# Maxima of the first unit sent through DRAM in two halves, and all steps of a planned kernel put in a new order

## The chip, the cores and the metric

The kernel runs on one core of one Trainium2 chip, as one program. The metric is the device time of one execution in microseconds (us). A core has five engines that run side by side, each its own instructions in a fixed order: TensorE (PE, matmuls), VectorE (DVE), ScalarE (ACT), GpSimd (POOL) and SyncE (SP, which here only issues DMAs). They wait for each other through semaphores.

## The reference

Four sequences (batches) of 1024 tokens by 128 features pass through eight blocks with residual adds; the last kind comes twice:

```python
x = x + _L0_attn_a_ref(_layernorm(x, axis=-1), ...)   # full attention, 16 heads of 8
x = x + _L0_ffn_ref(_layernorm(x, axis=-1), ...)
x = x + _L0_attn_b_ref(_layernorm(x, axis=-1), ...)   # causal, then local attention
x = x + _L0_ffn_ref(_layernorm(x, axis=-1), ...)
x = x + _L1_attn_a_ref(_layernorm(x, axis=-1), ...)   # window of 32, padded
x = x + _L1_ffn_ref(_layernorm(x, axis=-1), ...)      # 8 experts, 2 for each token
x = x + _L1_attn_b_ref(_layernorm(x, axis=-1), ...)   # window of 128 and 4 sinks
x = x + _L1_ffn_ref(_layernorm(x, axis=-1), ...)
```

Every attention ends in a softmax over the keys and a product with the values. The part that the change edits is in the full one:

```python
x_h = x.reshape(b, t, h, d).transpose(0, 2, 1, 3)
xw = jnp.einsum('bhtd,hde->bhte', x_h, w_att_val)
att = jnp.einsum('bhte,bhse->bhts', xw, x_h) / jnp.sqrt(jnp.asarray(d, x.dtype))
att = jax.nn.softmax(att, axis=-1)
...
o = jnp.einsum('bhts,bhsd->bhtd', att, vx)
```

## The kernel before

**Stages.** Batches are b0 to b3. Each goes through nine stages: full attention, ffn1, causal, local, ffn2, padded, moe1, sink, moe2. The stages of different batches overlap; the full attention of b0 and then that of b2 run in the first 500 us. In a moe stage the chosen tokens are gathered into 23 tiles of 128 slots (in DRAM, `scr_y`), and three matrices of an expert (`WB`, 384 KB a load) are loaded for each tile.

**One attention.** Full attention has four units of four heads, u0 to u3. For a unit the planner adds these steps:

- `load` (SP, L1819 and L1821): queries and keys from DRAM into one buffer each of the rings `QO` and `KO`, of four buffers each; 792 KB in four DMAs. It waits until the buffers' last readers are done.
- `maxima`: 32 steps "top", each four score matmuls (PE, L1102) and one maximum over them (DVE, L1532). 16 of them are for the unit's first two heads (hp 0), 16 for its last two (hp 1). Then `tops` (DVE, L1538, into `MTa`), `tops_turn` (a transpose on PE, L1109, and four operations on DVE that end in L1551, into `MTd`), `tops_out` (SP, L1839, `MTd` to DRAM, 24 KB) and `tops_in` (SP, L1848, two DMAs from DRAM into three more rows of `QO`). So the scores come out with their maximum taken off.
- `attend`: two halves (of the queries), each 16 steps "scores" (four matmuls on PE, L1122, and one exponential on ACT, L1295) and eight products with the values (PE, L1139). Each half ends with an ACT copy into `OB` (L1301) and a `divide` (PE L1149, DVE).

Tops and scores share a ring of three pairs of PSUM banks (`RB`). So maxima of the next unit run between scores of this one, one top taken with every score or two; a "pure stretch" of tops is one in which PE has no scores of the unit before left.

**What sets the order.** A planner (`Plan`, `streams`) takes the steps one by one with costs written into the code, and writes a fixed list for each engine. The tables `LEADS` (by stage) and `URGENT` (by kind of step) shift how early a step wants to be taken; `SHORT` and `WORTH` weigh which engine's steps go first and a step's use of a ring. On the chip each engine runs its list in order, and a waiting instruction holds up all behind it. That holds for the queue of SP too, which issues the loads, `tops_out`, `tops_in`, the loads of `WB`, and `zero` (L1855), one DMA of 1518 KB for each batch that clears `scr_y`. The sink attention of a batch (in the last quarter of the program) has units of the same steps on other shapes; its first top of a unit comes with mask matmuls (L1082).

## Time and profile before

| | |
|---|---|
| median of three runs | 2473.16 us (2466.74 to 2474.1) |
| profiled execution | 2472.5 us, span 2470.7 us |
| mean granted TensorE clock | 0.947 of full |
| PE busy | 2166.9 us, 88% of the span |
| DVE busy | 1653.9 us, 67% |
| ACT busy | 1440.0 us, 58% |
| POOL busy | 661.4 us, 27% |

The span runs from the first to the last instruction; the device time of the same execution is 1.8 us longer. A busy share is an average over stages: in the first 340 us DVE (maxima) and ACT (exponentials) work beside PE, and in the last 600 us PE waits for weights and for other engines at times.

### The profile page before, as it was taken

What the parts mean: (1) busy time and instruction counts of PE and PEld (TensorE: products, weight loads), DVE (VectorE), ACT (ScalarE), POOL (GpSimd) and SP (SyncE); (2) the same over time, 40 slices, a digit from 0 to 9 for tenths busy, and PEclk for the clock granted to TensorE, in tenths of its full rate; (3) what the DMA queues carried; (4) which work ended last, traced back from release to release, by engine and by line L of the source; (5) the groups of instructions that cost most, each with busy time, mean ns of one, the idle gap of its engine ahead of it and who ended that gap; (6) DMA issues with size and microseconds to landing.
All of it is one profiled execution on the core that took longest, in us unless ns stands there. A gap on an engine that the chain in (4) does not pass through costs nothing.

```text
span 2470.7 us, 61917 instructions
## 1 busy us (share of the span) xinstructions
PE 2166.9 (88%) x25853; PEld 1229.8 (50%) x25874; DVE 1653.9 (67%) x3651; ACT 1440.0 (58%) x2121; POOL 661.4 (27%) x597
## 2 busy tenths in 40 slices
PE   5588898789988999999898998899989889989987
PEld 2111231133322433423565446767857788766886
DVE  7888788776688777413745357675667576676545
ACT  1177657667887578799665774455344334344432
POOL 2400010020010202011233333433435364233563
PEclk8599999899999999999999999999999899989999
DMA  5600100111011111111222135535334666324576
GB/s 163 232 15 29 40 13 17 40 47 31 25 51 50 52 32 54 31 50 31 66 74 72 22 103 153 153 88 156 117 84 122 208 208 194 95 85 125 175 231 208
DMA packets 156238, 231.06 MB, mean 94 GB/s; under 512 B 19504, under 2 KB 79408, under 8 KB 155704
## 3 DMA queue, kind: packets, MB, share of 16 engines
q1 hardware_dynamic: 140952, 202.69, 28.1%
...
## 4 chain that ended last, share of the span: by engine, by line
PE 50%; DVE 19%; DMA 11%; ACT 7%; issue 6%; POOL 4%; SPq 3%; ACTq 0%; DVEq 0%; POOLq 0%
PE PS L1139 11%; DVE MS L1532 11%; PE PS L1188 6%; PE PS L1122 6%; ACT PT L1295 6%; PE PS L1102 5%; DMA scr_y<-XN,SL 3%; PE PS L1205 3%; PE PS L1089 3%; PE PS L1001 2%; PE PS L1011 2%; PE PS L972 2%; DMA WB<-in_mW 2%; PE PS L1082 2%; POOL scr_y L1756 2%
## 5 line engine op out<-in xcount | busy, mean ns | idle before, releaser
L1295 ACT ACTIVATE PT<-PS 128x1024 f32<-128x1024 f32 (+3 forms) x1216 | 1026.8, 908 | 399.5 <-PE PS L1122 392.0
L1532 DVE TENSOR_REDUCE MS<-PS 128x2 f32<-128x1024 f32 (+4 forms) x736 | 787.8, 1099 | 236.1 <-PE PS L1102 232.7
L1139 PE MATMUL PS<-PT,VA 128*9 128x512 f32 (+9 forms) x6720 | 571.3, 438 | 8.0 <-ACT PT L1295 6.2
L1122 PE MATMUL PS<-QO,KO 51*64 51x512 bf16 (+11 forms) x6304 | 444.4, 311 | 44.9 <-ACT PT L1295 16.1
L1102 PE MATMUL PS<-KO,QO 48*64 48x512 bf16 (+2 forms) x3520 | 302.9, 340 | 84.0 <-DVE MS L1532 70.8
L1122 PEld LDWEIGHTS PS<-QO,KO 51*64 51x64 bf16 (+3 forms) x6304 | 185.8, 107 | 238.7 <-ACT PT L1295 84.8
L1188 PE MATMUL PS<-SG,WB 128*128 128x128 f32 x2208 | 286.7, 283 | 16.8 <-DMA WB<-in_mW 14.4
L1102 PEld LDWEIGHTS PS<-KO,QO 48*64 48x64 bf16 (+1 forms) x3520 | 131.5, 107 | 337.4 <-DVE MS L1532 186.4
L1188 PEld LDWEIGHTS PS<-SG,WB 128*128 128x128 f32 x2208 | 269.1, 197 | 24.9 <-DMA WB<-in_mW 16.5
L1764 POOL DMA_INDIRECT scr_o<-SG,TO x184 | 181.5, 986 | 248.8 <-ACT SG L1337 226.0
L1317 ACT ACTIVATE HM<-PS 128x384 f32<-128x384 f32 x184 | 90.2, 490 | 224.9 <-PE PS L1188 224.9
L1139 PEld LDWEIGHTS PS<-PT,VA 128*9 128x9 f32 (+3 forms) x6720 | 127.0, 90 | 177.0 <-issue 121.8
L1089 PE MATMUL PS<-c_half 64*64 64x128 bf16 (+4 forms) x2560 | 170.3, 286 | 43.9 <-ACT PT L1295 15.3
L1654 DVE SCALAR_TENSOR_TENSOR HM<-HM,PS 128x384 f32<-128x384 f32 x184 | 101.2, 550 | 123.7 <-ACT HM L1317 123.2
L1205 PE MATMUL PS<-W,HM 128*128 x1104 | 160.4, 285 | 19.8 <-DVE HM L1656 9.8
L1756 POOL DMA_INDIRECT scr_y<-XN,SL x128 | 124.6, 974 | 194.1 <-DMA scr_y<-XN,SL 93.1
L1704 POOL MEMSET VA<- 128x32 f32 (+2 forms) x20 | 3.8, 190 | 643.7 <-PE PS L1139 643.7
L1089 PEld LDWEIGHTS PS<-c_half 64*64 64x64 bf16 x2560 | 65.5, 105 | 194.7 <-ACT PT L1295 96.2
L1205 PEld LDWEIGHTS PS<-W,HM 128*128 128x128 f32 x1104 | 139.9, 195 | 30.9 <-issue 29.6
L1301 ACT ACTIVATE OB<-PS 128x512 f32<-128x512 f32 x144 | 84.8, 599 | 92.5 <-PE PS L1139 89.5
L1561 DVE RECIPROCAL RC<-PS 128x16 f32<-128x16 f32 x144 | 36.3, 252 | 148.0 <-PE PS L1149 147.7
L1234 ACT ACTIVATE XT<-PS 128x512 f32<-128x512 f32 (+2 forms) x128 | 71.6, 593 | 90.0 <-PE PS L972 89.7
(166 smaller groups left out, 2377.1 us busy)
## 6 DMA issues: line engine op xcount, KB each, us to landing
...
```

Of the source, the lines that this page charges most:

```text
L1089: mm(pb[64 * c:64 * c + 64, h2, at:at + copies * width], C["identw"][r, :], rows, start=i == 0, stop=False, skip_group_check=True)
L1102: p = mm(pb[c:c + n, h2, at:at + kn], q[:, 128 * tt + c:128 * tt + c + n], k[:, k0:k0 + kn], start=not masked, stop=True, skip_group_check ...
L1122: p = mm(pb[c:c + n, h2, at:at + tn], k[:, k0 + c:k0 + c + n], q[:, t0:t0 + tn], start=not masked, stop=True, skip_group_check=masked)
L1139: p = mm(bank[32 * h:32 * h + D + 1, c0:c0 + tn], va[0:kn, :], pt[0:kn, h % 2, at:at + tn], start=s["first"] and j == 0, stop=s["last"] an ...
L1188: p = mm(pb[:, k, 128 * c:128 * c + 128], wt[:, at:at + 128], y, start=True, stop=True)
L1205: p = mm(RA[s.use["bank"].i][:, 0:128], hm[:, 128 * c:128 * c + 128], W3[:, bass.ds(first + 128 * c, 128)], start=c == 0, stop=c == 2)
L1295: e = activation(pt[0:r, :, a:b], ps[0:r, :, a:b], ACT.Exp, scale=s["A"].scale)
L1317: activation(HM[s.use["hm"].i][:, :], RB[s.use["bank"].i][:, 0, 0:DW], ACT.Tanh, scale=0.5).then_inc(S["up_tanh"], 1)
L1532: v.tensor_reduce(to, got, AX.X, ALU.max).then_inc(S["top"], 1)
L1654: last(v.scalar_tensor_tensor(hm, hm, 1.0, pb[:, 0, 0:DW], ALU.add, ALU.mult))
L1756: p.indirect_dma_start(scr_y[b], bass.IndirectOffsetOnAxis(ap=SL[b][:, c, i:i + 1], axis=0), XN[:, i, 0:ROW], None).then_inc(S[s.signals[" ...
L1764: p.indirect_dma_start(scr_o[b], bass.IndirectOffsetOnAxis(ap=TO[b][:, t:t + 1], axis=0), SG[s["yt"].i][:, at:at + 128], None).then_inc(S[ ...
```

## The change

It has two parts. First, for unit u0 of b0 alone, the maxima are sent in two halves: after the 16 tops of two heads come a `tops`, a `tops_turn`, a `tops_out` and a `tops_in` of their own, on 16 rows instead of 32, and then the same again for the other two heads. Scores of a pair of heads wait only for their own `tops_in`. All other units wait as before. Second, the tables have other numbers, so that the order of steps on all engines is another one.

```diff
--- before.py
+++ after.py
@@ -17,11 +17,11 @@
 RS8 = float(8.0) ** -0.5
 INF = float("inf")
 HOP = 200.0
-LEADS = dict(full=(1132, -776, 406, -1439), ffn1=(-3117, -525, 2830, 2001), causal=(1089, -1943, -1344, -1890), local=(-1543, 777, -158, 647), ffn2=(-197, 3580, -615, -1022), padded=(-948, -510, -413, -182), moe1=(2339, -1699, 271, -906), sink=(556, 567, -1777, 1297), moe2=(2401, -2034, -4275, -134))
...
-SHORT = dict(pe=2339.0, act=1281.0, dve=653.0, pool=2521.0, sp=24300.0)
+LEADS = dict(full=(715, -319, 616, -1226), ffn1=(-3511, -187, 2610, 2331), causal=(1741, -1760, -1442, -1611), local=(-1557, 1080, 559, 503), ffn2=(277, 3502, -765, -1049), padded=(-858, -449, -354, -310), moe1=(2599, -1691, 527, -724), sink=(348, 595, -1796, 1382), moe2=(2448, -2203, -3913, -26))
...
+SHORT = dict(pe=100.0, act=1260.0, dve=653.0, pool=3206.0, sp=24467.0)
 ISSUE = 500.0
-SWITCH, WORTH = 95.0, 285706.0
+SWITCH, WORTH = 95.0, 80724.0
 ENGINES = ("pe", "act", "dve", "pool", "sp")
 SLOT_TILES, GROUP, ROW = 23, 4, 132
 STAGES = ("moe1", "moe2")
@@ -459,16 +459,24 @@
                     s.use["tk"].give(s["top"])
                     top.append(s["top"])
                     U["read"].append(s["top_mm"])
-            s = add("tops", [("dve", 200, "tops")], dict(top=top), dict(mt=MT), A=A, ms=ms)
-            ms.give(s["tops"])
+                if U["halves"]:
+                    U["m"].append(sent_tops(A, U, top, ms, hp, hp == 1))
+                    top = []
+            if not U["halves"]:
+                U["m"] = [sent_tops(A, U, top, ms, None, True)] * 2
+
+        def sent_tops(A, U, top, ms, hp, last):
+            s = add("tops", [("dve", 200, "tops")], dict(top=top), dict(mt=MT), A=A, ms=ms, hp=hp)
+            if last:
+                ms.give(s["tops"])
             mt = s.use["mt"]
-            s = add("tops_turn", [("pe", 200, "tops_mm"), ("dve", 1150, "tops_split")], dict(tops=[s["tops"]]), dict(bank=RA), mt=mt)
+            s = add("tops_turn", [("pe", 200, "tops_mm"), ("dve", 1150, "tops_split")], dict(tops=[s["tops"]]), dict(bank=RA), mt=mt, hp=hp)
             s.use["bank"].give(s["tops_split"])
-            s = add("tops_out", [("sp", ISSUE, "")], dict(tops=[s["tops_split"]], m=state["m"]), b=b, dmas=lambda s: [("m_out%s" % b, 1, 2200, 100)])
+            s = add("tops_out", [("sp", ISSUE, "")], dict(tops=[s["tops_split"]], m=state["m"]), b=b, hp=hp, dmas=lambda s: [("m_out%s" % b, 1, 2200, 100)])
             mt.give(s["dma"])
-            s = add("tops_in", [("sp", 2 * ISSUE, "")], dict(m=[s["dma"]]), A=A, U=U, b=b, dmas=lambda s: [("q_in%s" % U["qo"].i, 2, 2200, 200)])
+            s = add("tops_in", [("sp", 2 * ISSUE, "")], dict(m=[s["dma"]]), A=A, U=U, b=b, hp=hp, dmas=lambda s: [("q_in%s" % U["qo"].i, 2, 2200, 200)])
             state["m"] = [s["dma"]]
-            U["load"] = U["load"] + [s["dma"]]
+            return s["dma"]
 
         def attend(A, U, va, v_ready, o):
             done, read = [], []
@@ -482,7 +490,7 @@
                     for hp in range(2):
                         s = add("scores", [("pe", score_mms([x[3] for x in g["blocks"]], A.tiled, masked), "scores"),
                                            ("act", sum(on_act(2 * (x[2] - x[1])) for x in g["exps"]), "exp")],
-                                dict(load=U["load"]), dict(bank=RB, pt=PT, **chain) if po is None else dict(bank=RB, pt=PT),
+                                dict(load=U["load"] + U["m"][hp:hp + 1]), dict(bank=RB, pt=PT, **chain) if po is None else dict(bank=RB, pt=PT),
                                 leaves=dict(PT=1 - hp), A=A, U=U, g=g, hp=hp, po=po, behind=behind, mode=mode(A.tiled))
                         po, behind, fc = s.use.get("po", po), s.use["pt"], s.use.get("fc", fc)
                         s.use["bank"].give(s["exp"])
@@ -518,7 +526,7 @@
                     takes["o"] = O
                 s = add("load", [("sp", ISSUE * n, "")], dict(q=state["q"][:u + 1], k=state["k"][:u + 1], ones=ones_in if A.tops else []), takes, A=A, b=b, u=u, o=o,
                         dmas=lambda s, n=n: [("q_in%s" % s.use["qo"].i, n, 2000, 1300)])
-                U = dict(u=u, qo=s.use["qo"], qo2=s.use.get("qo2"), ko=s.use["ko"], load=[s["dma"]], read=[])
+                U = dict(u=u, qo=s.use["qo"], qo2=s.use.get("qo2"), ko=s.use["ko"], load=[s["dma"]], read=[], m=[], halves=A.name == "full" and b == 0 and u == 0)
                 if "rest" in state:
                     state.pop("rest")([s["dma"]])
                 if A.name == "full" and u == 2:
@@ -852,6 +860,11 @@
              half=("identb", "identw", "mC", "mL", "mA", "mB", "mBt", "mBt1", "below", "onesb"))
 
 
+def heads_of(s):
+
+    return slice(0, 32) if s["hp"] is None else slice(16 * s["hp"], 16 * s["hp"] + 16)
+
+
 def program(nc, d, places, out, scr, scr_m, scr_y, scr_o):
     ctx = ExitStack()
     with ctx:
@@ -1106,7 +1119,9 @@
             def tops_turn(s):
                 w.wait_all(s.needs["tops"])
                 w.wait_all(s.use["bank"].after)
-                nc.tensor.transpose(RA[s.use["bank"].i][0:32, 0:128], MTa[:, :], ident[:, :]).then_inc(S["tops_mm"], 1)
+                r = heads_of(s)
+                n = r.stop - r.start
+                nc.tensor.transpose(RA[s.use["bank"].i][0:n, 0:128], MTa[:, 0:n], ident[:, :]).then_inc(S["tops_mm"], 1)
 
             def scores(s):
                 w.wait_all(s.needs["load"])
@@ -1534,21 +1549,24 @@
             def tops(s):
                 w.wait_all(s.needs["top"])
                 w.wait_all(s.use["mt"].after)
+                r = heads_of(s)
                 if s["A"].name == "full":
-                    v.tensor_tensor(MTa[:, :], MS[:, :, 0], MS[:, :, 1], ALU.max).then_inc(S["tops"], 1)
+                    v.tensor_tensor(MTa[:, 0:r.stop - r.start], MS[:, r, 0], MS[:, r, 1], ALU.max).then_inc(S["tops"], 1)
                 else:
                     v.tensor_copy(MTa[:, :], MS[:, :, 0]).then_inc(S["tops"], 1)
 
             def tops_turn(s):
                 w.wait_ge("tops_mm", s.signals["tops_mm"].value)
-                top = RA[s.use["bank"].i][0:32, 0:128]
-                last(v.tensor_scalar(MTd[:, 0, :], top, -1.0, None, ALU.mult))
-                settled()
-                last(v.scalar_tensor_tensor(MTc[:, :], top, -1.0, MTd[:, 0, :], ALU.mult, ALU.subtract))
-                settled()
-                last(v.tensor_copy(MTd[:, 1, :], MTc[:, :]))
-                settled()
-                v.tensor_tensor(MTd[:, 2, :], MTc[:, :], MTd[:, 1, :], ALU.subtract).then_inc(S["tops_split"], 1)
+                r = heads_of(s)
+                n = r.stop - r.start
+                top = RA[s.use["bank"].i][0:n, 0:128]
+                last(v.tensor_scalar(MTd[0:n, 0, :], top, -1.0, None, ALU.mult))
+                settled()
+                last(v.scalar_tensor_tensor(MTc[0:n, :], top, -1.0, MTd[0:n, 0, :], ALU.mult, ALU.subtract))
+                settled()
+                last(v.tensor_copy(MTd[0:n, 1, :], MTc[0:n, :]))
+                settled()
+                v.tensor_tensor(MTd[0:n, 2, :], MTc[0:n, :], MTd[0:n, 1, :], ALU.subtract).then_inc(S["tops_split"], 1)
 
             def divide(s):
                 A, u, half = s["A"], s["U"]["u"], s["half"]
@@ -1836,14 +1854,18 @@
             def tops_out(s):
                 w.wait_all(s.needs["tops"])
                 w.wait_all(s.needs["m"])
-                eng.dma_start(scr_m[s["b"]].rearrange("a r t -> r a t"), MTd[:, :, :]).then_inc(S[s.signals["dma"].name], 16)
+                r = heads_of(s)
+                eng.dma_start(scr_m[s["b"]][:, r, :].rearrange("a r t -> r a t"), MTd[0:r.stop - r.start, :, :]).then_inc(S[s.signals["dma"].name], 16)
 
             def tops_in(s):
                 A, U, got = s["A"], s["U"], S[s.signals["dma"].name]
                 w.wait_all(s.needs["m"])
                 rows_ = scr_m[s["b"]].rearrange("a (h t) c -> a h (t c)", t=8)
                 for i in range(2):
-                    if A.tiled:
+                    if s["hp"] is not None:
+                        c0 = A.K + 64 * i
+                        eng.dma_start(QO[U["qo"].i][c0:c0 + 3, s["hp"], :], rows_[:, 2 * s["hp"] + i, :]).then_inc(got, 16)
+                    elif A.tiled:
                         c0 = A.K + 64 * i
                         eng.dma_start(QO[U["qo"].i][c0:c0 + 3, :, :], rows_.rearrange("a (p r) c -> r a p c", r=2)[i]).then_inc(got, 16)
                     else:
```

**Place 1: TensorE at the start, b0.** `KO0,QO0` is u0 of b0 and `KO1,QO1` its u1; four L1102 (L1115 after) matmuls are one top; L1122 (L1137 after) on `QO0,KO0` are scores of u0. Before:

```order
L1102 MATMUL PS<-KO0,QO0 64x512 x72
L1212 MATMUL PS<-HOT,c_rest 128x128
L1109 MATMUL PS<-c_first,MTa 32x128
L1102 MATMUL PS<-KO1,QO1 64x512 x60
L1122 MATMUL PS<-QO0,KO0 64x512 x8
L1102 MATMUL PS<-KO1,QO1 64x512 x4
L1122 MATMUL PS<-QO0,KO0 64x512 x4
```

After:

```order
L1115 MATMUL PS<-KO0,QO0 64x512 x20
L1124 MATMUL PS<-c_first,MTa 16x128
L1115 MATMUL PS<-KO0,QO0 64x512 x52
L1124 MATMUL PS<-c_first,MTa 16x128
L1115 MATMUL PS<-KO1,QO1 64x512 x8
L1227 MATMUL PS<-HOT,c_rest 128x128
L1137 MATMUL PS<-QO0,KO0 64x512 x4
L1115 MATMUL PS<-KO1,QO1 64x512 x44
L1137 MATMUL PS<-QO0,KO0 64x512 x8
```

The transpose of the maxima is now two, and four scores of u0 stand after 2 tops of u1, the next eight after 11 more, where the first eight stood after 15.

**Place 2: TensorE from u2 to u3 of b0.** `MTa` is the transpose for the maxima of u3; `QO2,KO2` scores are u2's, `QO3,KO3` scores u3's, and the `KO0,QO0` tops are for u0 of b2. Before:

```order
L1122 MATMUL PS<-QO2,KO2 64x512 x8
L1139 MATMUL PS<-PT2,VA0 9x512 x2
L1139 MATMUL PS<-PT3,VA0 9x512 x2
L1109 MATMUL PS<-c_first,MTa 32x128
L1122 MATMUL PS<-QO2,KO2 64x512 x8
L1139 MATMUL PS<-PT4,VA0 9x512 x2
L1139 MATMUL PS<-PT5,VA0 9x512 x2
L1102 MATMUL PS<-KO0,QO0 64x512 x4
L1122 MATMUL PS<-QO2,KO2 64x512 x4
```

After:

```order
L1154 MATMUL PS<-PT4,VA0 9x512 x2
L1154 MATMUL PS<-PT5,VA0 9x512 x2
L1124 MATMUL PS<-c_first,MTa 32x128
L1115 MATMUL PS<-KO0,QO0 64x512 x8
L1164 MATMUL PS<-c_first,OB1 128x128 x4
L1115 MATMUL PS<-KO0,QO0 64x512 x36
L1137 MATMUL PS<-QO3,KO3 64x512 x4
L1115 MATMUL PS<-KO0,QO0 64x512 x4
```

Before, scores of u2 stand on both sides of the transpose and go on behind it; now none are left, and 11 tops in a row stand between the transpose and the first scores of u3 (between u1 and u2 it is 7 in the same way, and 11 again between u2 and u3 of b2, where it was 5).

**Place 2 on the queue of SP.** `QO2` and `KO2` loads are for u2 of b2 and `QO3`, `KO3` for its u3; `scr_y2` is the zeroing. Before:

```order
L1839 DMA scr_m<-MTd 32x3x128
L1848 DMA QO3<-scr_m 3x2x1024 x2
L1819 DMA QO2<-scr_q_full 48x2x1024
L1821 DMA KO2<-scr_k_full 51x2x1024
L1819 DMA QO2<-scr_q_full 48x2x1024
L1821 DMA KO2<-scr_k_full 51x2x1024
L1855 DMA scr_y2<-HM0 128x23x132
L1819 DMA QO3<-scr_q_full 48x2x1024
```

After:

```order
L1837 DMA QO2<-scr_q_full 48x2x1024
L1839 DMA KO2<-scr_k_full 51x2x1024
L1837 DMA QO2<-scr_q_full 48x2x1024
L1839 DMA KO2<-scr_k_full 51x2x1024
L1858 DMA scr_m<-MTd 32x3x128
L1877 DMA scr_y2<-HM0 128x23x132
L1870 DMA QO3<-scr_m 3x2x1024 x2
L1837 DMA QO3<-scr_q_full 48x2x1024
```

The `tops_out` for u3 (to `QO3`) stood ahead of the loads for `QO2`; it now stands behind them, and the zeroing has come between it and its `tops_in`. A zeroing waits by the code until the loads for its batch's u2 have landed (`loaded`); here those are the `QO2` loads just ahead. In b2 it is likewise for u3: loads of `QO2`, `tops_out`, zeroing, `tops_in`, where it was `tops_out`, the loads, `tops_in`, and then the zeroing.

**Place 3: TensorE in the sink attention of b1, from its first unit to its second.** The tops on `KO3` wait for a load into buffers that the last scores before them leave. Before:

```order
L1122 MATMUL PS<-QO1,KO2 4x256 x2
L1122 MATMUL PS<-QO3,KO2 4x256 x2
L1139 MATMUL PS<-PT3,VA1 17x512 x2
L1139 MATMUL PS<-PT2,VA1 17x512 x2
L1139 MATMUL PS<-PT4,VA1 17x256 x2
L1139 MATMUL PS<-PT5,VA1 17x256 x2
L1149 MATMUL PS<-c_first,OB1 128x128 x4
L1149 MATMUL PS<-c_first,OB0 128x128 x4
L1082 MATMUL PS<-c_half 128x128 x2
L1102 MATMUL PS<-KO3,QO1 128x128 x2
L1082 MATMUL PS<-c_half 128x256 x2
```

After:

```order
L1137 MATMUL PS<-QO1,KO2 128x128 x4
L1095 MATMUL PS<-c_half 128x512 x2
L1137 MATMUL PS<-QO2,KO2 128x256 x2
L1137 MATMUL PS<-QO2,KO2 128x128 x4
L1154 MATMUL PS<-PT1,VA1 17x256 x2
L1154 MATMUL PS<-PT3,VA1 17x256 x2
L1095 MATMUL PS<-c_half 128x512 x2
L1137 MATMUL PS<-QO1,KO2 128x256 x4
L1095 MATMUL PS<-c_half 128x512 x2
L1137 MATMUL PS<-QO2,KO2 128x256 x4
L1095 MATMUL PS<-c_half 128x128 x2
L1115 MATMUL PS<-KO3,QO0 128x128 x2
```

Before, the last scores that read `QO1` stand just ahead of the first top of the next unit, with products and divides alone between. Now the top reads `QO0`; its last scores stand 20 rows ahead, and four steps of scores are among what is between.

## Rows read from the trace of the kernel before

**Rows 1.** The page, busy time by engine.
```profile
PE 2166.9 (88%) x25853; PEld 1229.8 (50%) x25874; DVE 1653.9 (67%) x3651; ACT 1440.0 (58%) x2121; POOL 661.4 (27%) x597
```

**Rows 2.** Windows: stretch, length, then busy time of each engine, clock, DMA.
```profile
110.00:340.00 230.00, 196.03 (x1909) 55.34 (x1909) 191.01 (x219) 152.26 (x166) 8.88 (x7) 0.96 0.12 37
...
860.00:1120.00 260.00, 245.97 (x3233) 94.49 (x3231) 128.37 (x227) 220.68 (x290) 35.28 (x27) 0.99 0.17 42
...
1885.00:2175.00 290.00, 253.06 (x2410) 220.11 (x2408) 188.83 (x509) 107.52 (x222) 130.15 (x126) 0.92 0.54 163
...
2220.00:2470.70 250.70, 217.79 (x1951) 194.06 (x1953) 147.49 (x470) 97.95 (x203) 116.26 (x123) 0.95 0.61 182
```

**Rows 3.** Timeline of ScalarE (ACT): first exponentials, and ends of six halves.
```profile
110.94 3.22 ACT L1295 ACTIVATE PT<-PS 128x1024 f32<-128x1024 f32 x3 [49.32 <-PE PS L1122]
...
154.41 0.60 ACT L1301 ACTIVATE OB<-PS 128x512 f32<-128x512 f32 x1 [1.44 <-PE PS L1139]
...
283.88 0.60 ACT L1301 ACTIVATE OB<-PS 128x512 f32<-128x512 f32 x1 [1.50 <-PE PS L1139]
...
408.13 0.60 ACT L1301 ACTIVATE OB<-PS 128x512 f32<-128x512 f32 x1 [1.17 <-PE PS L1139]
...
426.61 0.60 ACT L1301 ACTIVATE OB<-PS 128x512 f32<-128x512 f32 x1 [1.21 <-PE PS L1139]
...
447.21 0.60 ACT L1301 ACTIVATE OB<-PS 128x512 f32<-128x512 f32 x1 [1.20 <-PE PS L1139]
...
479.24 0.60 ACT L1301 ACTIVATE OB<-PS 128x512 f32<-128x512 f32 x1 [1.52 <-PE PS L1139]
```

**Rows 4.** Timeline and chain: last unit of batch 2, from its maxima to its scores.
```profile
442.75 0.28 DVE L1551 TENSOR_TENSOR MTd<-MTc,MTd 32x128 bf16<-32x128 f32 x1
...
443.06 0.31 SPq L1839 DMA_DIRECT2D scr_m<-MTd  x1
...
446.12 1.43 SPq L1848 DMA_DIRECT2D QO<-scr_m  x2
...
446.86 7.52 DMA QO<-scr_m
...
454.43 1.07 PE L1122 MATMUL PS<-QO,KO 51*64 51x512 bf16 x8 [4.47 <-DMA QO<-scr_m]
```

**Rows 5.** Timeline and chain: first unit of batch 2, the same way.
```profile
281.15 10.46 DVE L1532 TENSOR_REDUCE MS<-PS 128x2 f32<-128x1024 f32 x9
...
281.67 0.31 SPq L1821 DMA_DIRECT2D KO<-scr_k_full  x1
282.02 0.35 SPq L1839 DMA_DIRECT2D scr_m<-MTd  x1
...
282.02 7.98 DMA scr_m<-MTd
...
290.77 2.41 DMA QO<-scr_m
...
293.22 1.07 PE L1122 MATMUL PS<-QO,KO 51*64 51x512 bf16 x8 [3.41 <-DMA QO<-scr_m]
```

**Rows 6.** DMA issues (KB each, us to landing), and SP's timeline around a zeroing.
```profile
scr_y<-HM SPq DMA_DIRECT2D x4, 1518.0 KB, 7.7
...
scr_m<-MTd SPq DMA_DIRECT2D x40, 24.0 KB, 1.8
...
239.58 0.30 SPq L1821 DMA_DIRECT2D KO<-scr_k_full  x1
247.59 0.38 SPq L1855 DMA_DIRECT2D scr_y<-HM  x1
```

**Rows 7.** Windows: the five us behind the gap of rows 4.
```profile
455.00:460.00 5.00, 4.30 (x36) 0.70 (x32) 2.36 (x2) 2.96 (x3) 0.00 (x0) 0.50 1.10 288
```

**Rows 8.** Waits of PE from 1885 to 2225 us: total, times, longest.
```profile
PE PS L1188 <- DMA WB<-in_mW: 11.3, 3, 4.9
PE PS L1082 <- DMA KO<-scr_k_sink: 8.3, 3, 3.4
```

More of the change, by code:

```diff
@@ L22 @@
-SHORT = dict(pe=2339.0, act=1281.0, dve=653.0, pool=2521.0, sp=24300.0)
+LEADS = dict(full=(715, -319, 616, -1226), ffn1=(-3511, -187, 2610, 2331), causal=(1741, -1760, -1442, -1611), local=(-1557, 1080, 559, 503), ffn2=(277, 3502, -765, -1049), padded=(-858, -449, -354, -310), moe1=(2599, -1691, 527, -724), sink=(348, 595, -1796, 1382), moe2=(2448, -2203, -3913, -26))
+URGENT = dict(back=-1052, biased=-1184, combine=1236, consts=3504, dest=-4253, divide_causal=-3548, divide_full=-949, divide_local=393, divide_padded=-1048, divide_sink=-4275, down=1593, experts_in=-1237, gate_exp=-3019, gate_w=-1504, k_padded=-2470, kv_global=1968, latent=-1094, load_causal=1549, load_full=-5813, load_local=3044, load_padded=-130, load_sink=539, mbd=-2827, mixed=-311, narrow=2257, norm=-590, ones=-1251, ones_rows=10, out=-1089, padding=1020, product_causal=-3134, product_full=3160, product_local=1643, product_padded=-4588, product_sink=-242, project_causal=1771, project_full=-3180, project_local=-3302, project_padded=1363, project_sink=2335, q_global=-2980, qk_rstd=-4107, qk_scaled=-2772, qk_squares=1653, qkv=1087, ranks=-2422, residual=1919, route=3703, rows_in=1482, rstd=722, scaled=-1933, scaled_dirs=-1387, scatter=-426, scores_causal=960, scores_full=-1762, scores_local=3958, scores_padded=-1764, scores_sink=-2488, slot_load=2695, slot_turn=1240, split_all=1420, split_hi=5065, split_lo=-1629, split_out_causal=87, split_out_full=-2146, split_out_local=1670, split_out_padded=-2246, split_out_sink=5837, squares=-3924, stats=10, store=550, top_full=-54, top_padded=-640, top_sink=564, tops_full=755, tops_in_full=6932, tops_in_padded=-1313, tops_in_sink=-3221, tops_out=5137, tops_padded=4635, tops_sink=-791, tops_turn=1958, turn=1256, turn_add=2068, turn_mul=3061, up=-488, v_full=785, v_padded=192, weights=-1812, widen=929, with_h=2811, zero=584)
```

1 line of the change is left out of this document (removed).

## The prediction

> **What bounds the kernel now.** I read the page, then the windows, then the timelines of three engines in the full attention, then PE's waits in the last quarter. PE is busy 88% of the span [rows 1], so time is won where it stands still and lost where it is made to. The windows show four kinds of stretch [rows 2]. From 110 to 340 us (full attention of b0, start of b2) DVE is busy 191.03 of 230 us, PE 196.03 and ACT 152.26: maxima, scores and exponentials mesh closely, and none has much to spare. From 860 to 1120 PE is busy 245.97 of 260: 14.0 us idle in all. From 1885 to 2175 it is 253.06 of 290 and from 2220 to the end 217.79 of 250.7: 36.9 and 32.9 us idle. In all other stretches the rows of the two orders are the same, so a shift passes through them unchanged.
>
> What one half costs is read from ACT's copies into `OB` [rows 3]. The six halves from 154.41 to 283.88 us took 129.47 us and hold 93 tops (counted in PE's order), so 21.58 us with 15.5 tops; the half from 408.13 to 426.61 took 18.48 with 10. That makes 0.563 us for a top and 12.85 us for the rest: T(n) = 12.85 + 0.563 n while scores and tops mesh. Without scores a top costs more: nine maxima took 10.46 us [rows 5], 1.16 each, with DVE as the pace.
>
> The half from 447.21 to 479.24 took 32.03 us [rows 3]. It is the one case in b2 in which u2's scores are used up before u3's maxima are back. The chain [rows 4]: the last maxima operation ends at 443.03, `tops_out` goes at 443.06, `tops_in` at 446.12, behind the four loads for the next batch, lands after 7.52, and PE has its first score at 454.43, 11.4 us after 443.03. ACT stood too. Five of the half's 18 tops lay in the gap; T(13) is 20.2, so the gap cost 11.8 us, the round trip and 0.4 more. That holds the cold restart: the five us behind the gap ran at a granted clock of 0.50 [rows 7], the lower of the two levels, after PE had waited 4.47 us.
>
> The second case is u0 of b2 [rows 5]: loads ahead of `tops_out`. It goes at 282.02, takes 7.98 to land (1.8 is the median [rows 6]), `tops_in` takes 2.41, and the score comes at 293.22, 12.1 us after DVE's last operation (281.15, when the next reduction begins). So loads ahead of either hop cost some 5 to 6 us.
>
> **The change part by part.**
>
> *The halves at the start.* Scores of u0 come 2 tops of u1 earlier: four alone after 2 tops, all others after 13 instead of 15. At 1.16 that is 2.3 us off the 110.94 at which ACT starts [rows 3]. The first half now has 14 tops beside it instead of 16 (1.1 us off), the second 14 instead of 13 (0.6 on). The added set is one PE transpose, five DVE operations of some 0.25 us (1.2 us in all, from the 0.28 of the one in rows 4), three DMA issues on SP; DVE is the pace there, so I count 1.2 in full. Sum: -1.6 us. The early scores of two heads alone bring little, since the next eight stand behind 11 tops in PE's queue whatever has landed.
>
> *b0, from u1 to the end of u3.* Six halves now hold 94 tops, of which 7 and 11 stand in two pure stretches. Outside them 76 are left: 6 x 12.85 + 0.563 x 76 = 119.9 us, 9.6 less than 129.47. The first gap (u1 to u2, 7 tops) has the form of rows 5, loads ahead of `tops_out`: 12.1 + 0.4 = 12.5. Its lower bound is the tops alone, 7 x 1.16 = 8.1. The second (u2 to u3, 11 tops, 12.8 us at 1.16) has loads ahead of `tops_out` and the zeroing ahead of `tops_in`. The zeroing waits for those loads to land, as it did from 239.58 to 247.59, 8.0 us, and then takes 7.7 [rows 6]. What is behind the waiting zeroing on SP is `tops_in`, and for that all of u3's scores wait, with ACT. If `tops_in` lands no sooner than the zeroing, the round trip is 12.1 + 0.4 (issue) + 7.7 - 2.4 = 17.8, and the gap 18.2; if it were free to pass, 12.8, the tops' own pace. I take 18.2, because `tops_in` behind loads landed only after 7.52 instead of 2.41 [rows 4, 5]. So b0: -9.6 + 12.5 + 18.2 = +21.1, between +11.3 and +23 (with 20 for the second gap).
>
> The Trainium skill, in "DMA: Bandwidth & Descriptors", section "Queues, rings and completion order", says that a DMA engine takes the descriptors of a ring in their order, and that SP has one row of rings. By it `tops_in` can't pass the zeroing where both use an engine, which speaks against the change and for 18.2; were it not so, the second gap would be 5.4 us less here and in b2. Rows 4 and 5 agree with it.
>
> *b2.* Eight halves hold 124 tops against 122, with 11 in the pure stretch between u2 and u3 against 5: outside it 113 against 117, -2.3 us. The gap grows from 11.8 to 18.2, since loads are now ahead of `tops_out` and the zeroing ahead of `tops_in`: +6.4. Sum +4.1; at the lower bound (12.8) -1.3.
>
> *860 to 1120 us.* The order differs in detail, PE's work is the same, and 14.0 us of idle time are left to move. I count +1, between -3 and +6.
>
> *The sink attention and the last moe.* PE waited for `KO<-scr_k_sink` three times, 8.3 us in all, and for weights three times, 11.3 us [rows 8]. The new order puts scores or maxima between a buffer's last reader and the next unit's first top; four such steps are over 3 us of PE work, so I take the 8.3 off. Of the weights' waits one of 3.4 goes, as three of the weight loads now stand ahead of the slot loads on SP. What is moved takes some of its places in other waits; I put 4 us on. Sum -7.7, between -13 (no new waits, one more us at the tail) and +2 (new waits as long as the old). The last three slot tiles of b2 go behind those of b3 in moe2; PE's work is the same, and I count nothing.
>
> **Sum.** -1.6 + 21.1 + 4.1 + 1 - 7.7 = +16.9 us against the profiled execution of 2472.5 us, which stands 0.7 under the median of 2473.16: 2490 us.
>
> **Rivals.**
>
> *The tail wins (faster, 0.15).* Place: PE's idle time after 1885 us, 36.9 + 32.9 = 69.8 us [rows 2]. If the new order meshes moe, sink and weights well there, it gives back more than the first 500 us cost. Speaking for it: rows 8 show that 19.6 us of it are DMA waits, which order alone can hide. Against: most other waits are chains between engines whose steps are the same. With the front at its lower bound (-1.6 + 11.3 - 1.3 + 1 = +9.4) and 19.6 off it is -10: 2463 us. It decides from the point where the tail gives back more than the front costs plus 7.4 us.
>
> *The round trips are hidden (no change, 0.25).* The pure stretches then cost only their own tops: +9.4 at the front, -7.7 behind: +2, 2475 us. For it: `scr_m<-MTd` has a median of 1.8 us. Against: both cases in which scores ran out show 11 to 12 us. The deciding number is the time from the last maxima operation of u3 to its first score, under 13 us.
>
> *The tail gives nothing back (slower still, 0.15).* The front as forecast, the new waits at the back as long as the old ones: +16.9 + 9.7 = +26.6, 2500 us.
>
> *The tables alone matter and the halves do nothing* is part of the forecast: -1.6 is within what can be told.
>
> **How the numbers follow.** The forecast (0.45) is +16.9, its own range +8 to +22. I take within 0.3%, 7.4 us, as what a measurement of this kernel can tell from no change. The range of 8 in 10 leaves out the outer part of the fastest rival and of the slowest: 2467 to 2502 us. Faster by over 0.3%: 0.14; within: 0.24; slower: 0.62.
>
> **What the profile after would show.** ACT's first exponential at about 109 us. In b0 the distance of two `OB` copies over a change of unit is over 28 us twice, first for u2, then for u3, and over 32 in b2 for u3; granted clock 0.50 right behind each. SP's zeroing issued some 8 us after the loads, `tops_in` just behind it and landing in 8 us or more. From there a shift of over 20 us that stays the same up to 860 us and up to 1885. In the sink attention no more waits on `KO<-scr_k_sink` of 2 us for the units of b1 and b3 with the new order. What would make it wrong: u3's scores within 13 us of its maxima; halves outside the gaps that take longer than T(n), for u2's second half holds 25 tops, 29 us at DVE's pace if none lie in the gap; or a tail that loses or wins over 10 us.

## The result and the profile after

The changed kernel takes 2504.89 us (median of four runs, 2501.34 to 2506.48) against 2473.36 us: 1.0132 of before, 95% interval 1.0110 to 1.0153, so 31.5 us slower. I had forecast 2490 us, at most 2502. The span of the profiled execution grew from 2470.7 to 2501.5 us.

First the page, where PE's busy time is what it was [rows 1]; all that was added is waiting:

```profile
PE 2164.9 (87%) x25853; PEld 1226.1 (49%) x25875; DVE 1662.5 (66%) x3656; ACT 1439.2 (58%) x2121; POOL 663.4 (27%) x597
```

The windows of the same stretches as [rows 2], each moved by the shift at that place (columns as there). PE's idle time is 44.7 us of 248 in the first, where it was 34.0 of 230, 19.0 instead of 14.0 in the second, 34.0 instead of 36.9 in the third and 40.1 instead of 32.9 in the last; between these two it is 7.9 of 50, where it was 2.6 of 45:

```profile
108.00:356.00 248.00, 203.34 (x1912) 55.70 (x1912) 193.31 (x219) 151.65 (x165) 10.59 (x7) 0.90 0.11 34
...
879.00:1140.00 261.00, 241.96 (x3133) 92.43 (x3121) 129.95 (x227) 217.12 (x284) 35.28 (x27) 0.99 0.15 39
...
1905.00:2195.00 290.00, 256.03 (x2423) 223.66 (x2428) 188.50 (x506) 110.98 (x228) 133.51 (x128) 0.94 0.54 164
2195.00:2245.00 50.00, 42.12 (x415) 29.85 (x420) 31.97 (x108) 18.98 (x24) 10.15 (x8) 0.90 0.23 75
2245.00:2501.50 256.50, 216.41 (x1943) 194.46 (x1946) 150.60 (x483) 96.61 (x202) 120.25 (x127) 0.94 0.60 179
```

ScalarE's copies into `OB`, one at the end of each half, as in [rows 3]:

```profile
130.22 0.60 ACT L1316 ACTIVATE OB<-PS 128x512 f32<-128x512 f32 x1 [1.44 <-PE PS L1154]
...
151.06 0.60 ACT L1316 ACTIVATE OB<-PS 128x512 f32<-128x512 f32 x1 [1.17 <-PE PS L1154]
...
191.55 0.60 ACT L1316 ACTIVATE OB<-PS 128x512 f32<-128x512 f32 x1 [1.17 <-PE PS L1154]
...
222.39 0.60 ACT L1316 ACTIVATE OB<-PS 128x512 f32<-128x512 f32 x1 [1.17 <-PE PS L1154]
...
244.25 0.60 ACT L1316 ACTIVATE OB<-PS 128x512 f32<-128x512 f32 x1 [1.17 <-PE PS L1154]
...
280.00 0.60 ACT L1316 ACTIVATE OB<-PS 128x512 f32<-128x512 f32 x1 [1.17 <-PE PS L1154]
...
300.49 0.60 ACT L1316 ACTIVATE OB<-PS 128x512 f32<-128x512 f32 x1 [1.17 <-PE PS L1154]
...
461.85 0.60 ACT L1316 ACTIVATE OB<-PS 128x512 f32<-128x512 f32 x1 [1.17 <-PE PS L1154]
...
498.15 0.60 ACT L1316 ACTIVATE OB<-PS 128x512 f32<-128x512 f32 x1 [1.17 <-PE PS L1154]
...
518.64 0.60 ACT L1316 ACTIVATE OB<-PS 128x512 f32<-128x512 f32 x1 [1.17 <-PE PS L1154]
```

The reader is to see three things. The first half ends 3.1 us earlier (130.22; before it was 133.32), and the second 3.4 (151.06 against 154.41 [rows 3]). Two steps over a change of unit are 30.8 and 35.8 us (191.55 to 222.39, 244.25 to 280.00), and in b2 one is 36.3 (461.85 to 498.15), where it was 32.0. At the end of b0's full attention the kernel is 16.6 us behind (300.49 against 283.88 [rows 3]), at the end of b2's 19.0. I followed the copies of both kernels to the end (times of before): 20.8 us behind at 720 us, 25.0 from 1150 to 1330 us, 21.4 at 1883, 30.8 at the end. So 20.8 us are lost in the front and 4.2 between 860 and 1140; 3.6 come back between 1330 and 1883, where ScalarE's order is the same in both kernels, and 9.4 are lost behind. The last two are only as good as one execution each: run 1 and run 4 below have the same order from about 860 us on, and the distance of their traces still grows from 20.4 us at 1330 to 35.2 at 1812. Behind 1330 us the ratios decide.

The second gap of b0, on SP's queue, DVE and PE:

```profile
246.01 0.30 SPq L1858 DMA_DIRECT2D scr_m<-MTd  x1
251.51 0.38 SPq L1877 DMA_DIRECT2D scr_y<-HM  x1
251.94 4.43 SPq L1870 DMA_DIRECT2D QO<-scr_m  x2
...
245.91 12.52 DVE L1547 TENSOR_REDUCE MS<-PS 128x2 f32<-128x1024 f32 x11
...
259.42 0.64 PE L1137 MATMUL PS<-QO,KO 51*64 51x512 bf16 x4 [2.56 <-DMA QO<-scr_m]
```

`tops_out` goes at 246.01; the zeroing waits for the loads and goes at 251.51; `tops_in` goes behind it, and two issues take 4.43 us. The last maxima operation had ended at 245.9, and the first score comes at 259.42: 13.5 us. DVE took its eleven maxima in 12.52 us of these. The first gap, measured in the same way, is 9.4 us (192.9 to 202.2).

The granted clock in and behind that gap (windows, columns as in [rows 2]):

```profile
245.00:259.00 14.00, 6.59 (x48) 1.61 (x40) 13.78 (x17) 0.00 (x0) 0.00 (x0) 0.58 0.53 145
259.00:264.00 5.00, 3.60 (x28) 0.83 (x32) 2.45 (x2) 3.14 (x4) 0.00 (x0) 0.50 0.00 0
264.00:269.00 5.00, 5.00 (x40) 0.76 (x32) 1.52 (x2) 2.76 (x4) 0.00 (x0) 0.62 0.01 3
269.00:274.00 5.00, 4.71 (x52) 0.87 (x48) 3.38 (x3) 4.78 (x6) 0.00 (x0) 1.00 0.00 0
```

In the stretch of maxima PE is busy 6.59 of 14 us and the clock falls; the next five us run at 0.50, the lower level, the next at 0.62, and only then is it back.

Where PE waits behind 1885 us. Before:

```profile
PE PS L1188 <- DMA WB<-in_mW: 13.1, 5, 4.9
PE PS L1082 <- DMA KO<-scr_k_sink: 10.1, 4, 3.4
PE PS L1205 <- ACT SG L1312: 8.4, 4, 2.9
...
PE PS L972 <- DVE XN L1399: 2.6, 2, 2.1
```

After (L1095 is the old L1082, L1203 the old L1188, L985 the old L972, L1220 the old L1205):

```profile
PE PS L985 <- DVE XN L1414: 12.1, 3, 5.7
PE PS L1203 <- DMA WB<-in_mW: 9.2, 5, 4.5
...
PE PS L1203 <- ACT SG L1327: 4.5, 1, 4.5
PE PS L1095 <- DMA QO<-scr_m: 4.4, 2, 3.9
PE PS L1203 <- DVE MS L1547: 4.0, 2, 2.1
PE PS L1095 <- DMA KO<-scr_k_sink: 3.3, 2, 2.2
...
PE PS L1220 <- ACT SG L1327: 3.0, 3, 2.0
PE PS L1095 <- DVE MS L1547: 2.1, 4, 0.6
```

The waits for `KO<-scr_k_sink` and `WB` fell by 6.8 and 3.9 us, but those for `XN` grew by 9.5, those for `QO<-scr_m` (4.4) are new, and those for the maxima (`MS`) grew by 5.1, from 1.0 to 6.1. Those for ScalarE's `SG` only changed place: one of 4.5 us is new, and in all they fell from 9.8 to 8.8. PE's idle time from 1885 us to the end was 72.5 us; from 1906.4, the same place in the changed kernel, it is 81.9.

The longest new one, on POOL, DVE and PE:

```profile
2309.43 0.96 POOL L1774 DMA_INDIRECT scr_y<-XN,SL  x1 [17.43 <-DVE SL L1658]
...
2351.13 2.36 DVE L1414 TENSOR_SCALAR XN<-X,MV,RS 128x128 f32<-128x128 f32 x8 [6.11 <-DMA scr_y<-XN,SL]
...
2353.55 1.97 PE L985 MATMUL PS<-c_first,XN 128*128 128x128 f32 x8 [5.69 <-DVE XN L1414]
```

POOL's first scatter of b1 (`XN` into `scr_y`) waits 17.43 us for its slots. Its last one is issued at 2348.72, since copies back of b2 stand between. The layer norm of b3 writes the same one buffer `XN`, so DVE starts it at 2351.13, after 6.11 us idle, and PE gets its transposes at 2353.55, after 5.69.

### The profile page after: what moved, and what is told of

Same layout as the page of the kernel before. It is cut to its first block, busy times and chain, and to the rows that moved or that the text cites. A ratio compares the mean times of both kernels' runs of the same rounds, so it can differ in the third digit from the quotient of the medians.

```text
span 2501.5 us, 61930 instructions
## 1 busy us (share of the span) xinstructions
PE 2164.9 (87%) x25853; PEld 1226.1 (49%) x25875; DVE 1662.5 (66%) x3656; ACT 1439.2 (58%) x2121; POOL 663.4 (27%) x597
## 4 chain that ended last, share of the span: by engine, by line
PE 45%; DVE 19%; DMA 13%; ACT 7%; issue 7%; POOL 6%; SPq 3%; ACTq 0%; DVEq 0%; POOLq 0%
PE PS L1154 10%; DVE MS L1547 9%; ACT PT L1310 6%; PE PS L1203 6%; PE PS L1137 6%; DMA scr_y<-XN,SL 5%; PE PS L1115 4%; PE PS L1220 3%; POOL scr_y L1774 3%; PE PS L1014 2%; PE PS L1024 2%; PE PS L985 2%; PE PS L1102 2%; DVE XN L1414 2%; DMA scr_m<-MTd 1%
## 5 line engine op out<-in xcount | busy, mean ns | idle before, releaser
L1154 PE MATMUL PS<-PT,VA 128*9 128x512 f32 (+10 forms) x6720 | 572.3, 439 | 10.7 <-ACT PT L1310 9.7
L1137 PE MATMUL PS<-QO,KO 51*64 51x512 bf16 (+10 forms) x6304 | 444.3, 311 | 59.5 <-ACT PT L1310 21.8
L1115 PE MATMUL PS<-KO,QO 48*64 48x512 bf16 (+2 forms) x3520 | 304.1, 345 | 84.0 <-DVE MS L1547 71.1
L1137 PEld LDWEIGHTS PS<-QO,KO 51*64 51x64 bf16 (+3 forms) x6304 | 186.0, 107 | 263.7 <-ACT PT L1310 105.9
L1203 PE MATMUL PS<-SG,WB 128*128 128x128 f32 x2208 | 287.2, 283 | 21.6 <-DMA WB<-in_mW 10.8
L1115 PEld LDWEIGHTS PS<-KO,QO 48*64 48x64 bf16 (+1 forms) x3520 | 129.5, 107 | 335.8 <-DVE MS L1547 194.7
L1203 PEld LDWEIGHTS PS<-SG,WB 128*128 128x128 f32 x2208 | 270.4, 198 | 28.2 <-issue 14.9
L1102 PE MATMUL PS<-c_half 64*64 64x128 bf16 (+4 forms) x2560 | 169.1, 285 | 41.4 <-ACT PT L1310 13.5
L1220 PE MATMUL PS<-W,HM 128*128 x1104 | 162.5, 288 | 14.8 <-DVE HM L1674 10.5
L1102 PEld LDWEIGHTS PS<-c_half 64*64 64x64 bf16 x2560 | 65.2, 105 | 183.7 <-ACT PT L1310 92.2
L1220 PEld LDWEIGHTS PS<-W,HM 128*128 128x128 f32 x1104 | 143.0, 199 | 23.9 <-issue 22.9
```

What stands on the lines that cost most here:

```text
L1102: mm(pb[64 * c:64 * c + 64, h2, at:at + copies * width], C["identw"][r, :], rows, start=i == 0, stop=False, skip_group_check=True)
L1115: p = mm(pb[c:c + n, h2, at:at + kn], q[:, 128 * tt + c:128 * tt + c + n], k[:, k0:k0 + kn], start=not masked, stop=True, skip_group_check ...
L1137: p = mm(pb[c:c + n, h2, at:at + tn], k[:, k0 + c:k0 + c + n], q[:, t0:t0 + tn], start=not masked, stop=True, skip_group_check=masked)
L1154: p = mm(bank[32 * h:32 * h + D + 1, c0:c0 + tn], va[0:kn, :], pt[0:kn, h % 2, at:at + tn], start=s["first"] and j == 0, stop=s["last"] an ...
L1203: p = mm(pb[:, k, 128 * c:128 * c + 128], wt[:, at:at + 128], y, start=True, stop=True)
L1220: p = mm(RA[s.use["bank"].i][:, 0:128], hm[:, 128 * c:128 * c + 128], W3[:, bass.ds(first + 128 * c, 128)], start=c == 0, stop=c == 2)
```

## The experiments

All kernels below but the last two are made in one way. Both orders are planned in the file, the old one and the new one; each engine's list is taken from the one or the other between cuts at which both orders have done the same steps; then the plan is run along these lists. `"a"` is the order of after, `"b"` that of before. The chips differ (before took 2513 us beside runs 1 to 4, 2519 beside 5 to 8, 2470 and 2471 beside the others), so runs are compared by their ratio to before on the same chip.

**1. The front alone (new_front).**

```diff
+PARTS = (('a', 0), ('b', 600))
```

> The changed kernel's order up to the end of the full attention of b2 (with the halves), and the order of before for all the rest. Theory A (the loss is made in two places that add up: about 20.8 us in the full attention, where the two profiles stand apart by 20.8 us at 720 us, and 10 us behind 860 us): 2473 + 20.8, some 2494 us, and the shift of 20.8 us against before stays the same to the end. Rival B (only the order behind 860 us is bad, and a late start there is caught up by waits that end at fixed work): under 2484 us. Rival C (the front carries all of it, since the stages behind it suffer from the shift itself): 2500 us or more.

Measured: 1.0087 (1.0065 to 1.0109), 2534.07 against 2513.18 us. Its copies into `OB` are 18 to 22 us behind those of the old order (run 4) from 527 to 1310 us. Theory A holds: the front loses some 20 us (21.8 by the ratio), and nothing behind it gives them back.

**2. The rest alone (new_back).**

```diff
+PARTS = (('b', 0), ('a', 600))
```

> The order of before, without halves, up to the end of the full attention of b2, and the changed kernel's order for all the rest. Theory A: no loss up to 860 us, then about 4 us from 860 to 1165 us and 6 behind 1885 us: some 2483 us. Rival B: 2500 us. Rival C: 2473 us, no difference.

Measured: 1.0069 (1.0048 to 1.0089). Up to 860 us its copies are within 1 us of those of run 4. The rest costs 17 us by the ratio, more than the 10 us that I had read from the two first traces, though the interval goes down to 12. The old order is not made up again: rival C falls.

**3. SP's queue as before (sp_before).** The changed kernel; in the full attention `tops_out` and `tops_in` stand ahead of the next loads again, and the zeroing behind.

```diff
+    other = spliced(a, b, (("b", 0), ("a", 600)))["sp"]
...
+    lists["sp"] = other
```

> The changed kernel with one edit: in the full attention SP's queue has the order of before (tops_out and tops_in of a unit ahead of the next loads, the zeroing behind tops_in); PE, DVE and ACT keep the changed order. Theory D (the prediction's: the round trip of the maxima is what the gaps cost, and loads and the zeroing ahead of the hops make it long): the second gap of b0 falls from 13.4 us to under 9, that of b2 likewise, and the kernel is 8 us or more faster than the changed one, 2496 us or less. Theory E (the stretches of 7 and 11 tops that DVE has to take at 1.14 us each are the bound, whatever the DMAs do): the gaps fall only to 8 and 12.5 us, and the kernel gains 1 to 4 us on the changed one, 2501 to 2504.

Measured: 1.0102 (1.0075 to 1.0130), where the changed kernel has 1.0131 to 1.0140, measured three times. The second gap of b0, with the clock behind it:

```profile
244.84 11.38 DVE L1636 TENSOR_REDUCE MS<-PS 128x2 f32<-128x1024 f32 x10
...
256.37 0.64 PE L1226 MATMUL PS<-QO,KO 51*64 51x512 bf16 x4 [0.58 <-DVE MS L1636]
...
244.00:257.00 13.00, 6.57 (x52) 1.73 (x44) 12.90 (x15) 0.00 (x0) 0.00 (x0) 0.69 0.21 64
257.00:262.00 5.00, 4.34 (x30) 0.78 (x28) 3.26 (x5) 3.88 (x4) 0.00 (x0) 0.50 0.57 168
262.00:267.00 5.00, 4.71 (x56) 1.01 (x52) 2.58 (x3) 3.77 (x4) 0.00 (x0) 0.94 0.67 152
```

The last maxima operation ends at 244.9, and the first score comes at 256.37, 11.5 us later. PE waits there for DVE (0.58 us) and for no DMA: the stretch of eleven tops is now the bound. The gaps are 7.0 and 11.5 us instead of 9.4 and 13.5; the maxima would be back sooner and help nobody. The clock is at 0.94 in the second five us behind the gap, where it was 0.62. At the end of b2's full attention this kernel is 6.5 us ahead of the changed one (512.16 against 518.64). So theory E names the bound: the gaps fell to its 8 and 12.5 us or a little less, not under 9. By that trace the DMAs cost 6 to 7 us, between the 8 or more that D asked and the 1 to 4 of E; by the ratios it is 7 to 10 us, but their intervals overlap, so the total does not settle between 6 and 8. Some 12.5 of the 19 us stay with SP's queue as it was. No run spread the maxima out again by themselves, so that these 12.5 us are the pure stretches is read from the trace.

**4. The halves in the old order (halves_only).**

```diff
+PARTS = (('b', 0),)
...
+            if key[1] < 0:
+                lists[e].insert(lists[e].index(last) + 1, key)
```

> The order of before on all engines, with the maxima of the first unit sent in two halves, the five extra DVE operations, the extra transpose and the extra DMAs put in where the changed kernel has them; PE takes the first scores after 15 tops of the next unit as before. Theory A (the loss is in the order, not in the halves): within 2 us of before, 0 to +1.5 by the extra DVE operations at the start. Rival F (the extra hops on SP's queue or in DRAM hold something up): 3 us or more over before, visible at the first exponential (110.94 us before).

Measured: 0.9996 (0.9978 to 1.0015). First and last copy of b0:

```profile
133.57 0.60 ACT L1404 ACTIVATE OB<-PS 128x512 f32<-128x512 f32 x1 [1.17 <-PE PS L1242]
...
284.14 0.60 ACT L1404 ACTIVATE OB<-PS 128x512 f32<-128x512 f32 x1 [1.50 <-PE PS L1242]
```

They stand 0.25 us behind those of before, at both ends. The steps put in are `tops`, `tops_turn`, `tops_out` and `tops_in` of the first two heads, each where "a" has it. They cost nothing that can be told; the interval would hide 4 us.

**5. The changed kernel beside the next three (after_again).**

> The changed kernel itself, unchanged in its order, on the chip of this call, as the measure for the three beside it. Ratio to before 1.013 as first measured; if front and back add up as on the chip of the first call (1.0087 and 1.0069), 1.0156.

Measured: 1.0140 (1.0115 to 1.0165), and beside the last three runs 1.0131 (1.0105 to 1.0156):

> The changed kernel in its own order again, as the measure for the run with the later turn beside it: ratio 1.013 to 1.014.

**6. Only 860 to 1165 us in the new order (mid_only).**

```diff
+PARTS = (('b', 0), ('a', 600), ('b', 1200))
```

> The order of before, with the changed kernel's order only between some 860 and 1165 us (local attention, ffn2 and their neighbours). Theory A: +4.2 us, the step between the two profiles there (20.8 to 25.0), ratio 1.0017. Theory G (the prediction's +1): 1.0004. Rival: the step is made by the shifted start alone, 1.000.

Measured: 1.0023 (1.0007 to 1.0039), 5.8 us by the ratio. Theory A; G's 1.0004 lies just outside the interval.

**7. Only the part behind 1865 us in the new order (tail_only).**

```diff
+PARTS = (('b', 0), ('a', 1500))
```

> The order of before up to some 1865 us, and the changed kernel's order from there on (sink attention, last moe stages). The prediction's theory H (waits for buffers and weights go away): 7.7 us faster than before, ratio 0.997. Theory A (waits moved and grew, as PE's stalls over 1.2 us behind 1885 us went from 41.2 to 48.6 us and the profiles part by 6 us more): 6 us slower, 1.0024.

Measured: 1.0035 (1.0015 to 1.0055): 8.8 us slower by the ratio, where my forecast had it 7.7 us faster. Front, middle and tail add up: 0.0087 + 0.0023 + 0.0035 = 0.0145, against 0.0140 for the whole.

**8. The halves used (early_scores).** The old order, the first score of u0 after 2 tops, the next after 13.

```diff
+            if n in (14, 15):
+                continue
...
+    slots += [tops[-1]] * 2
```

> The order of before with the halves of the first unit and the use that the change makes of them: first score of u0 after 2 tops of u1, the next after 13 instead of 15, and no other order changed (two tops move behind the first half's scores). Theory A (the halves give what the start shows, -3.1 us at the first copy into OB, and nothing else changes): 1 to 3 us faster than before, ratio 0.999 to 0.9995, all of it kept to the end. Rival: given back by the next half, which has two tops more: no difference by 154 us.

Measured: 1.0014 (0.9996 to 1.0031).

```profile
131.63 0.60 ACT L1426 ACTIVATE OB<-PS 128x512 f32<-128x512 f32 x1 [1.17 <-PE PS L1264]
...
156.95 0.60 ACT L1426 ACTIVATE OB<-PS 128x512 f32<-128x512 f32 x1 [1.44 <-PE PS L1264]
```

The first half ends 1.9 us earlier than in run 4 (133.57), the second 2.3 later (154.66), so it took 25.3 us instead of 21.1. Two more tops do not cost that. My edit set them down right at the change of halves, next to others, and the clock fell there. The window from 136 to 141 us, first in this run, then in run 4:

```profile
136.00:141.00 5.00, 4.81 (x34) 0.85 (x32) 2.81 (x5) 2.85 (x3) 0.00 (x0) 0.50 0.00 0
...
136.00:141.00 5.00, 4.65 (x49) 1.07 (x49) 3.92 (x10) 4.97 (x7) 0.00 (x0) 1.00 0.00 0
```

The rival (the gain is given back by the next half) was right for this run. It does not speak for the changed kernel, whose second half took 20.8 us and kept the gain (3.1 us at the first copy, 3.4 at the second).

**9 and 10. The tail in two parts (tail_first_part, tail_last_part).**

```diff
+PARTS = (('b', 0), ('a', 1500), ('b', 2190))   # first part
+PARTS = (('b', 0), ('a', 2190))                # last part
```

> The order of before, with the changed kernel's order only for the part from some 1885 us to 2185 us (moe1 of the last batches, sink attention, start of moe2), and again the order of before behind it. Theory J (the part that my forecast had right is here: waits for KO<-scr_k_sink shrink by some 5 us, but new waits for XN, SG and the maxima take as much): within 3 us of before, ratio 0.999 to 1.0012. Theory K (the new waits are mostly here): 1.003 or more.

> The order of before up to some 2185 us, and the changed kernel's order from there to the end (rest of the sink attention, moe2 of b1 and b3, last tiles of b2). Theory J (POOL takes the scatters of b1 into its slots later, mixed with the copies back of b2, so the layer norm of b3 waits for its one buffer XN and PE with it, 5.7 us in the changed kernel's trace, and b2's last three tiles no longer cover that wait): 5 to 9 us slower than before, ratio 1.002 to 1.0036, with a PE wait of 4 us or more for XN. Theory K: within 2 us of before.

Measured: 1.0105 (1.0085 to 1.0125) for the first. This one tells little, for the seam made a stall of its own:

```profile
2280.01 0.61 PE L1176 MATMUL PS<-c_half 128*128 128x256 bf16 x2 [17.08 <-DVE MS L1628]
```

PE stands 17 us behind the change of orders, in neither kernel's trace; without it some 9 us are left, and I do not build on them. The last part: 1.0042 (1.0025 to 1.0058), 10.3 us, with the wait for `XN`:

```profile
2329.43 1.97 PE L1066 MATMUL PS<-c_first,XN 128*128 128x128 f32 x8 [7.07 <-DVE XN L1495]
```

It is 7.07 us here, in the old order of everything ahead of it. Theory J's numbers (5 to 9 us, a wait of 4 us or more for `XN`) hold for the last part; whether that wait is the price is what runs 11 and 12 ask.

**11. The scatters of b1 together (scatters_first).** POOL alone is changed.

```diff
+    pool[own[0]:own[-1] + 1] = [k for k in part if k[0] == "scatter"] + [k for k in part if k[0] != "scatter"]
```

> The changed kernel with one edit on POOL's queue: the eight scatters of b1 in moe2 stand together, ahead of the six copies back of b2, and of the rstd of b3 where two came behind it. Nothing moves on the other engines. Theory J: the layer norm of b3 gets XN up to 10 us earlier, PE's wait of 5.7 us before its transposes of XN goes, and the kernel is 4 to 6 us faster than the changed one (0.998 of it: some 1.012 to before where the changed kernel had 1.014). Rival L (the wait is only moved: the copies back come later, the buffers SG with them, and PE waits for ScalarE there): no difference to the changed kernel, 1.014.

Measured: 1.0191 (1.0175 to 1.0208), 0.005 to 0.006 over the changed kernel. PE's wait for `XN` is gone, and there is another:

```profile
2340.40 1.65 PE L1309 MATMUL PS<-W,HM 128*128 x6 [18.25 <-ACT SG L1416]
```

The copies back of b2 came later, with them the buffers `SG`, and PE stood 18.25 us for ScalarE. Theory J fell and rival L was right, at a far higher price than it had named.

**12. The layer norm of b3 behind three more tiles (turn_later).**

```diff
+    for engine, j, i in (("dve", norm, 0), ("act", turn, 1), ("pe", turn, 0)):
...
+        row[at:end] = ahead + rest
```

> The changed kernel with one edit in moe2: the layer norm of b3, its turn on PE and ScalarE's copies of it stand behind three more slot tiles of the batches before. POOL's queue is as it was. Theory J (XN comes late through POOL's queue, and what costs is that PE, DVE and ScalarE stand in order behind it while tiles are ready): the PE wait of 5.7 us for XN falls under 1 us, the wait at about 2384 to 2404 us stays, and the kernel is 3 to 6 us faster than the changed one beside it. Rival L (the tiles' copies back or the route of b3 are the next bound): under 2 us faster, with a new wait behind.

Measured: 1.0182 (1.0158 to 1.0205), against 1.0131 for the changed kernel on the same chip. The wait for `XN` (7.50 us in the changed kernel's trace there) is gone, and the slot tiles come 5.9 us earlier than there at 2353 us; at 2379 they are 3.2 us late, and the end comes 4.8 us late. In between:

```profile
2351.58 1.64 PE L1316 MATMUL PS<-W,HM 128*128 x6 [3.06 <-DVE HM L1770]
...
2369.34 0.44 PE L1277 MATMUL PS<-MASK,c_half 128*128 128x64 bf16 x8 [3.16 <-DVE MASK L1723]
```

waits for the tile's own `HM` and for the masks of b3's route, which is now late. L again.

**13 and 14. Each part of the change by itself, planned anew (replan_halves, replan_tables).**

```diff
+globals().update(BEFORE, HALVES=True)     # 13
+globals().update(AFTER, HALVES=False)     # 14
```

> The kernel of before with the first part of the change alone: halves for the first unit, tables of before, the planner free. Its order up to about 390 us is that of the changed kernel, row for row. Theory M (the halves themselves, by way of the planner, make the pure stretches; the tables have no part in them): copies into OB as in the changed kernel, 16 to 17 us behind before at the end of b0's full attention, and a ratio of 1.007 or more, with what the re-ordered rest adds or takes. Rival (the tables make the stretches): no shift at 300 us.

> The kernel of before with the second part of the change alone: the changed tables, no halves, the planner free. Its order up to about 380 us is that of before. Theory M: no shift at 300 us; the ratio is that of the re-ordered rest alone, which the changed kernel's own rest puts at 1.0058 to 1.0069; but the order behind 400 us is another one again, so 0.998 to 1.012.

Measured: 1.0815 (1.0782 to 1.0849) for the halves with the old tables, 1.0855 (1.0833 to 1.0876) for the new tables without the halves. The end of b0's full attention, halves first:

```profile
302.25 0.60 ACT L1400 ACTIVATE OB<-PS 128x512 f32<-128x512 f32 x1 [1.17 <-PE PS L1238]
```

Tables:

```profile
284.69 0.60 ACT L1400 ACTIVATE OB<-PS 128x512 f32<-128x512 f32 x1 [1.42 <-PE PS L1238]
```

302.25 and 284.69 us, against 283.88 before and 300.49 after: the halves make the front's loss by way of the planner, and the tables have no part in it. Over the whole program each does six times as badly as the two together (1.0132). The tables of before fit the order of before alone, and the new tables fit the order with the halves alone. That I had not expected by far (0.998 to 1.012 for the tables).

## Why the prediction was wrong

The direction and the first reason were right, the size was half. By its steps:

- *The halves at the start: -1.6 us.* ScalarE's first copy came 3.1 us earlier, the second 3.4. Right in kind, and too small.
- *b0: +21.1.* Measured 16.6 with the start, so 20.0 without it. The mechanism is the forecast one: two gaps, first u2, then u3. The round trips were priced too high, 12.1 and 17.8 us where 9.4 and 13.5 were measured: from the issue of `tops_out` behind loads to that of `tops_in` it was 6.1 and 5.9 us and not the 7.98 of [rows 5]. That `tops_in` does not pass the zeroing was right: the zeroing landed 7.5 us after its issue, and PE's score comes 7.9 us after it. The Trainium skill's rule from "DMA: Bandwidth & Descriptors", section "Queues, rings and completion order", of descriptors taken in the ring's order, agrees with that. Priced too low, by some 7 us, were the halves around the gaps, with the clock at 0.50 and 0.62 for ten us behind the second; I had counted 0.4 us a gap for that. The two errors nearly cancel, so that the sum came close is luck. My counts of tops were off as well: in the traces the six halves hold 88 before and 91 after, not 93 and 94, and with these my own sum gives +18.0.
- *Which of both bounds the gap.* I put the price on the DMAs and held the tops' own pace for the lower bound. Run 3 shows it nearer to the lower bound: 12.5 of 19 us stay when the DMAs are out of the way.
- *b2: +4.1.* Measured 2.4, and 1.8 more by 720 us.
- *860 to 1120 us: +1, between -3 and +6.* 4.2 in the traces, 5.8 by run 6. Inside the range, not at its likely place. *The stretches between:* a shift was to pass unchanged; from 1330 to 1883 us it fell by 3.6, in single traces.
- *The sink attention and the last moe: -7.7.* This is the step that failed. What it takes off is right: 6.8 us of waits for `KO<-scr_k_sink` and 3.9 for weights went, 10.7 of the 11.7 forecast. What it puts on is the failed term: "What is moved takes some of its places in other waits; I put 4 us on." PE's idle time there grew by 9.5 us with 10.7 taken off, so some 20 us came on and not 4: 9.5 for `XN`, 5.1 for maxima, 4.4 for `QO<-scr_m`, and small ones. The sum was +9.4 in the traces and +8.8 by run 7 (3.8 to 13.9), some 17 us from the forecast, more than the 14.6 us by which the total was off; the other misses are small and partly cancel. Its bounds (-13 to +2) did not hold it: the upper one took new waits to be about as long as the old ones at most, with no row for that.
- I had also counted nothing for the last three tiles of b2. They would have been ready work at the place of the 5.69 us wait; no run put them back alone, so this is only argued. Runs 11 and 12 show that neither of the two moves that took this wait away took its price off.
- The rivals: the tail's win had the wrong sign. The hidden round trips put the front at +9.4, with u3's first score within 13 us; it came after 13.5, and the front lost 20.8. The nearest was the last, "the tail gives nothing back", 2500 us.

What stays open: which of the tail's new waits carries its 9 us, why the slots of b1 come so late in the new order that POOL waits 17.43 us for them, and which moves between 860 and 1165 us cost the 4 to 6 us there. By the traces PE's waits for exponentials and maxima there are each a little longer, and none stands out.
